# Slot parameters normalised in the embedding, expert row scales in two rounds, attention's masks and first loads behind the gathers, the recurrence output's loads inside the recurrence

## What is computed

```python
h = base_weight[ids]; h = where(id is tuned, train_weight[row], h)          # embedding
h = h + attention(layernorm(h))          # 12 heads of 16, column 0 masked for all rows but 0
h = h + switch_ffn(layernorm(h))
# test-time-training layer, 12 heads of 64, chunks of 16 tokens:
for each of the 32 chunks:               # W, b are the state of each head
    grad = ln_l2_bwd(k @ W + b, v - k);  W -= (last_eta * k).T @ grad;  b -= ...
    out = q + layernorm(q @ W - (eta * tril(q k.T)) @ grad + b - (eta * tril) @ grad)
h = h + (layernorm(out) * gelu(x @ wg)) @ wo
# soft mixture of 32 experts with 32 slots each:
xn   = l2norm(layernorm(h));  phin = scale * phi / max(norm of phi over its 192 rows, 1e-12)
d_w  = softmax(xn @ phin over slots);  c_w = softmax(xn @ phin over all 1024)
h = h + c_w @ experts(d_w.T @ xn)
```

## Time and profile before

| | us |
|---|---|
| median of 3 runs | 1601.47 |
| lowest, highest | 1600.15, 1617.8 |
| the profiled execution, device time | 1609.5 |
| its span in the trace | 1607.7 |

### The profile page before, as it was taken

How to read it: one execution, slowest core, us unless ns; L and a number is a source line. 1 busy time by engine, 2 the same in 40 slices (tenths; PEclk the granted TensorE clock), 3 DMA queues, 4 the chain that set the end, 5 groups by cost and what they waited for, 6 DMA issues and landing times. The chain is left out here.

```text
span 1607.7 us, 28934 instructions
## 1 busy us (share of the span) xinstructions
PE 1337.4 (83%) x10025; PEld 930.0 (58%) x10025; DVE 904.1 (56%) x2168; ACT 758.6 (47%) x1536; POOL 359.1 (22%) x378
## 2 busy tenths in 40 slices
PE   0939999699489993989999948989758887898979
PEld 0503333346257772677777736767654433798879
DVE  4448885412577771777686849787845766000001
ACT  0406556221234441788797925767632332333333
POOL 7230000000167773344343420000001223000000
PEclk9959999659789997899999979999966999899989
DMA  2351120000313334333333343212023000399941
GB/s 54 94 92 51 54 57 21 23 1 0 89 42 119 119 119 124 91 106 103 111 98 109 100 105 85 57 48 55 1 67 81 0 1 0 94 261 244 262 111 39
DMA packets 113496, 132.12 MB, mean 82 GB/s; under 512 B 27871, under 2 KB 99278, under 8 KB 113272
## 3 DMA queue, kind: packets, MB, share of 16 engines
...
...
## 5 line engine op out<-in xcount | busy, mean ns | idle before, releaser
L561 DVE TENSOR_REDUCE mx<-bank 128x1 f32<-128x512 f32 x192 | 119.6, 681 | 35.1 <-PE bank L483 34.8
L621 ACT ACTIVATE PT<-bank 128x1024 f32<-128x1024 f32 x96 | 94.3, 1022 | 85.6 <-PE bank L499 84.9
L2181 POOL TENSOR_TENSOR m_cw<-m_E,m_f 128x1024 f32<-128x1024 f32 x16 | 45.1, 2817 | 381.9 <-DVE m_f L2126 381.9
L2266 DVE TENSOR_TENSOR x_eo<-bank,b 128x192 f32<-128x192 f32 x32 | 11.4, 357 | 173.1 <-PE bank L2243 173.1
L2232 PE MATMUL bank<-slT,w 96*128 x768 | 97.6, 287 | 13.3 <-DMA b<-in_m_b 9.3
L1552 POOL TENSOR_SCALAR r_grD<-gr 32x192 f32<-32x192 f32 x128 | 68.5, 535 | 173.1 <-DVE gr L1455 152.1
L1334 PE MATMUL bank<-r_grD,ek 128*128 128x256 f32 x384 | 105.2, 412 | 0.0
L2232 PEld LDWEIGHTS bank<-slT,w 96*128 96x128 f32 x768 | 93.8, 201 | 17.8 <-issue 17.8
L2254 ACT ACTIVATE x_g<-bank,w 128x128 f32<-128x128 f32 x192 | 53.0, 375 | 105.5 <-PE bank L2232 105.5
L483 PE MATMUL bank<-K,Q 97*128 97x512 bf16 x192 | 70.0, 418 | 28.2 <-POOL K L636 24.9
L1334 PEld LDWEIGHTS bank<-r_grD,ek 128*128 128x128 f32 x384 | 70.9, 198 | 13.7 <-issue 0.7
...
## 6 DMA issues: line engine op xcount, KB each, us to landing
...
```

What stands on the lines that cost most here:

```text
L561: v.tensor_reduce(mx[u % 2][:, j // 4, j % 4:j % 4 + 1], slot(f"A{u}.{j}"), AX.X, ALU.max).then_inc(*dve.did(f"max{u}.{j}"))
L621: a.activation(PT[kt % 2][:, 2 * hp:2 * hp + 2, :], STB[s % 2][:, :, :], ACT.Exp, scale=DH ** -0.5)\
```

## The change

**Embedding.** Two loads of `m_phi` and one of `m_scale` are issued behind the weights, and the normalisation of `phi` is done here with the same operations as before in dispatch (ACT squares and root, 16 matmuls, 8 spreading matmuls, four DVE products); the result is stored to a new DRAM tensor `phin_d`. DVE's part stands between `tuned` and `layer_norm(0)`. ACT takes one square root ahead, so that the table is loaded early. The first `train(0)` comes before `base(2)`. Behind its last gather POOL writes attention's mask rows. SP issues the 36 loads of attention's units 0 to 2 behind the stores of sequence 1 and ahead of those of sequences 2 and 3, and no longer waits at the end for the stores of the sequences to land (attention waits for them where it loads).

**Preparation and recurrence.** `W0`, `B0`, `g2` come as three whole loads in the preparation, and DVE centres them at its end. In the recurrence POOL fills two key tiles first instead of zeroing all four; PE and ACT start each half by itself. SP's loop is written out; the loads of steps past the end are gone but for one. SP loads there what the output needs: mask tables ahead of the steps, parameters behind step 0, three tiles behind steps 26 to 28, biases behind steps 27 to 30. DVE zeroes the output's tiles and builds its masks before the first step (before, POOL zeroed them, at the output's start).

**Dispatch.** SP loads `phin_d` instead of `m_phi`. Statistics and row scales are computed for sequence 0 alone and then for the other three; `units(1)` and `units(2)` move into the loop, to tiles 1 and 5.

The heart of the diff:

```diff
@@ embed, SP
+                for k in range(KC):
+                    sp.dma_start(phi[:, k, :], ins["m_phi"][k * DC:(k + 1) * DC, :]).then_inc(phi_in, 16)
+                sp.dma_start(scale[:, :], ins["m_scale"]...).then_inc(phi_in, 16)
...
+                for k in range(KC):
+                    sp.wait_ge(normed, k + 1)
+                    sp.dma_start(M["phin_d"][k * DC:(k + 1) * DC, :], phi[:, k, :]).then_inc(phi_out, 16)
                 for b in SB:
+                    if b == 2:
+                        sp.wait_ge(stored[0], 16 * 2 * QUADS)
+                        for u in C:
+                            attention_rows(sp, M, u)
...
-                for r in range(2):
-                    sp.wait_ge(stored[r], 16 * 2 * QUADS * B // 2)
+                sp.wait_ge(phi_out, 32)
@@ embed, DVE, behind tuned
+                v.wait_ge(rooted, 1)
+                v.tensor_scalar(size[:, :], size[:, :], FLOOR, None, ALU.max).then_inc(united, 1)
...
+                v.wait_ge(spread, 1)
+                for k in range(KC):
+                    for hf in range(2):
+                        cols = slice(hf * SL // 2, (hf + 1) * SL // 2)
+                        last = v.tensor_tensor(phi[:, k, cols], phi[:, k, cols], QK[hf][0:DC, :], ALU.mult)
+                    last.then_inc(normed, 1)
@@ embed, POOL
                 base(0)
                 base(1)
+                train(0)
                 base(2)
-                train(0)
@@ attention, PE
-                t_.wait_ge(masks, QUADS)
@@ ttt_recur, SP
-                with sp.Fori(0, STEPS // SPT) as sc:
+                for s in range(STEPS):
...
+                    if s + RING <= STEPS:
                         sp.wait_ge(*dve.at(f"gx1.{j}", sc))
                         targets(r, nx)
...
+                    if s + RING < STEPS:
                         sp.wait_ge(*pe.at(f"upd1.{j}", sc))
                         keys(r, nx)
...
+                    if s in (26, 27, 28):
+                        t = s - 26
...
+                            sp.dma_start(O["Wd"][t][rr, :, rr], M["W_d"][t, rr, :, 0, :]).then_inc(O["tiles_in"][t], 16)
+                            sp.dma_start(O["Gs"][t][:, hh, :], M["g_d"][0, hh, t * P:(t + 1) * P, :]).then_inc(O["tiles_in"][t], 16)
+                    if s in (27, 28, 29, 30):
+                        t = s - 27
...
+                                sp.dma_start(O["b6"][r0:r0 + HP, t, :, hh * E1:(hh + 1) * E1],
@@ ttt_recur, PE
-                t_.wait_ge(primed_k, 3)
-                t_.wait_ge(primed_w, 2)
-                before(0, 0).then_inc(first_z, 1)
+                t_.wait_ge(primed_k, 1)
+                t_.wait_ge(primed_w, 1)
+                before(0, 0).then_inc(first_z, 1)
@@ moe_dispatch, DVE
+                sizes(0, slice(0, TB))
                 units(0)
...
-                units(2)
+                sizes(1, slice(TB, TILES))
                 for i in I:
+                    if i == 1:
+                        units(1)
+                    if i == TB + 1:
+                        units(2)
```

445 lines of the change are left out of this document (228 added, 217 removed).

## The result

The changed kernel takes 1553.86 us (median of four runs, 1551.44 to 1560.38). The kernel before took 1606.73 us beside it (four runs, 1600.15 to 1617.8). The ratio is 0.9688, with a 95% interval of 0.9613 to 0.9764. The medians differ by 52.9 us. The two profiled executions took 1609.5 and 1560.38 us and differ by 49.1 us, where the prediction had 62.2.

A forecast was written before the change was run, and what follows sets the result against it. Five idle gaps of 5 to 25 us at block starts, adding in full, were taken as removable: 16.9 + 14.0 + 4.9 + 13.0 + 13.4 = 62.2 us. On the median 1601.47 that gave 1540 us, range 1532 to 1555.

The forecast's parts named there:

- The embedding's gain of 16.9: Embedding to attention's first matmul: sequences 5.5 us earlier, SP decides the end, first matmul at 87.3 instead of 104.2.
- the cost of 0 for the recurrence's steps: Recurrence loop: steps stay at 8.10 us, SP's added loads land in time; bound 1 us at each of five steps.
- Masks beside work: Embedding: POOL's mask memsets follow its last gather at about 52, done by 69, beside other work.
- 1.6 us a stretch: Embedding: memsets would stretch scalings of sequences 2 and 3 by 1.6 us each, sum unchanged since SP decides.
- Preparation, 0: Preparation's end: three DMAs and some 3.5 us of DVE work hidden under SP's last stores; 3.5 without that cover.
- Recurrence's start, 14.0: Recurrence block's start: tables land at 628, first variance at 631.1 instead of 645.60; gain 14.0, bounds 10 and 17.5.
- the bound of 10: Recurrence's start: lower bound of the gain, if tables come 4 us later behind 1.2 MB of state loads.
- Recurrence's end and output's start, 4.9 + 13.0: Recurrence ends at 934.3 instead of 939.24; output's first square comes 10.3 us into its block instead of 23.3.
- The upper bound, a higher granted clock: Output's start: gain up to 15, since after a short idle time PE's clock may still be at the higher level.
- Dispatch's start, 13.4: First logits 14.4 us sooner, less 1.0 for units(1); gain 10.6 if units(2) is not absorbed.
- the likeliest case: Whole kernel: the forecast itself, 1534 to 1546 us, chance 0.54.
- one start stays: Rival, chance 0.13: another wait replaces a removed one, likely at recurrence or output; price 10 to 13 us, 1552.

The follow-up runs named there:

- first pair: The first profiled executions of the kernel before and the changed kernel, no further edit: 1609.5 and 1560.38 us.
- before: The kernel without the change: median 1606.73 us beside the changed kernel.
- after: The kernel with the change described above and no further edit: median 1553.86 us, ratio 0.9688 against the kernel before.
- group 1: Runs on one chip: both kernels once more, masks moved back behind attention's block, and no normalisation of phi; the kernel before took 1614.58 us in one run.
- group 3: Runs on one chip: changed kernel once more (1566.09 us), padding in embedding gaps, row tables first, and all four edits together.
- groups 2, 4 and 5: Runs sharing a chip within each group: 2 gathers, masks, loads, padding; 4 added gathers, repeats, three mends; 5 three mends with padding, and the kernel before (1595.84 us).
- again_after: Changed kernel once more, no edit, second profile: 1563.52 us, ratio 0.9746 against the kernel before.
- masks_late: Changed kernel with the mask memsets back at the start of attention's block, PE waiting for them: 1586.52 us, ratio 0.9877.
- half_gathers: Changed kernel without the last eight of 32 gathers (tuned rows of sequences 2 and 3): 1550.15 us in one run.
- after_fourth: Changed kernel once more, no edit, beside the added-gathers run: 1548.83 us, ratio 0.97 against the kernel before.
- second pair: Two later profiles of the same two kernels, on two different chips; attention starts at 104.14 and 88.91 us, the difference sums to 49.6 us.
- gathers_attn: Changed kernel with 192 more gathers on POOL during attention, into a tile nobody reads: 1664.92 us, ratio 1.0443.
- idx_first: Changed kernel with the output's four mask-table loads ahead of targets and keys in the recurrence's block: 1556.74 us, ratio 0.9736.
- no_phi: Changed kernel without the normalisation of phi, so dispatch gets it unscaled: 1548.69 us, ratio 0.9638.
- pad32: Changed kernel with 32 unused one-column matmuls in the embedding, where PE waits for phi's squares: 1553.7 us, ratio 0.9788.
- pad_gaps: Changed kernel with two lots of 16 unused one-column, 16-row matmuls in gaps of the embedding: 1569.22 us, ratio 0.9787.
- best: Changed kernel with four edits: masks paced by sequence 3's scaling, attention loads split, padding in embedding gaps, mask tables first: 1561.2 us, ratio 0.9708.
- lean_pad: Changed kernel with masks paced, loads split, tables first, plus 32 unused matmuls at the end of the preparation: 1531.77 us, ratio 0.9606.
- loads_split: Changed kernel with attention's 36 loads split, 12 ahead of sequence 1's stores and 24 ahead of sequence 2's: 1548.03 us, ratio 0.9722.
- best_lean: Changed kernel with masks paced by sequence 3's scaling, loads split, tables first, no padding: 1535.94 us, ratio 0.9646.

## Why the prediction was right or wrong

**What failed, in short.** The gaps and their releasers were read rightly, and four of the five starts came as forecast or within 3 us. Two steps failed. The embedding's gain of 16.9, by which all sequences follow 5.5 us earlier in a chain, was absent in the first pair, where TensorE and ACT issue late by 15.6 us; why they do is open. And the cost of 0 for the recurrence's steps was 4.1 to 10.7 us. The gain of 10.7 us in the experts' stage, which no step had, covers part of this.

**What bounds the kernel.** Right: five gaps at block starts, in a row, each with its releaser. All five could be closed or shortened. What was wrong is that the work between them keeps its length.

**Embedding, 16.9 forecast: nearly right without the slow issue, absent in the first pair.** Without the slow issue it is 15.2 (104.14 to 88.91), with first matmul at 88.91 against the forecast's 87.3. SP decides, as the step said: loads to 79.17 (forecast 78.4), stores to 87.8 (86.7); the last 1.1 us are the meeting of the engines at the block's border, for which the step had 0.6. The last `phi` product ends at 28.25 (forecast 27.5). With the slow issue in both kernels the gain is 8.6 (112.89 to 104.25); with it in after alone it is nothing. The step that failed in the first pair is the sentence that the other sequences "follow in a chain" 5.5 us earlier: from about 31 us to 53, TensorE and ACT issue ever more slowly in the profile of after and in two of the five groups, and the first store comes at 60.04, not 48.19. There was no row for it, as the profile of before is of an execution without it. Between the two profiles of after, 11.9 us are there at the first store, 15.1 at the end of sequence 1's stores (76.9 against 61.8), and 15.6 at the first matmul (104.56 against 88.91).

What causes it stays open. In all four profiles of group 1, both of after and before among them, it is there, and so in group 3; it is in none of groups 2, 4 and 5, group 4 having run on the chip of group 3. Neither `phi`'s normalisation nor the masks bring it about, and before has it without either. It starts while the gathers are issued and ends at 52.8 to 56.1 us, about when the last has landed (53.1 to 53.4 by POOL's wait); more TensorE instructions in that stretch make it longer (26.55 us of ACT idle in the padded kernel). The two runs meant to vary the gathers fell into groups without it. The timed medians of after by group, 1563.5 and 1566.1 with it, 1548.8 without, fit its price, and so do those of before (1606.2 and 1603.7 with it, 1593.9 to 1595.1 without it, for a price of 8.7). The first pair doesn't fit in as well: before has 1606.7 with a profile that is free of it, and after 1553.9 with one that has it. The groups differ in their chips, too. So the medians suggest that it isn't an effect of profiling, but do not show it.

**Masks beside work.** The prediction placed them there at no cost. Without the slow issue it was right: they meet the scaling of sequence 3, hidden behind SP. With it they meet that of sequence 2, 6.58 us instead of 1.25, and 7.31 in again_after. That costs the stage 1.3 us by masks_late, so it is a small part of what the embedding lost; where POOL comes to the masks sooner, as in half_gathers, attention starts 4.4 us later than in the kernels beside it. The prediction's sentence from the Trainium skill (SBUF — State Buffer, practical consequences) expected 1.6 us a stretch, sized by one slow row of the dispatch loop. By the Trainium skill's rule itself, that the later engine waits for the whole instruction, four scalings can each wait for a memset of 1.80 us, 7.2 in all. The trace agrees with this reading of it: the four operations of after_fourth take 1.39, 1.94, 1.97 and 1.94 us. The 1.25 of masks_late agrees too; it was my sizing that was wrong.

**Preparation, 0.** Right in mechanism: DVE's last operation ends 14.3 us ahead of the recurrence's block in before and 10.6 in after, while POOL's ends 12.0 ahead in both. From attention's first matmul to the block it is 515.1 before and 514.3 after (515.0 and 516.0 in the second pair). This stretch of stages takes 508.9 to 516.9 us over 19 profiles, gathers_attn left aside, so a cost of a few us could not have been seen in its length.

**Recurrence's start, 14.0: 11.9.** Right in mechanism: DVE waits for SP's tables, the case that the bound of 10 was made of. The term mis-sized is the landing of the fourth table. Forecast at 628, it let DVE go on at 630.67: issued at 623.26, it let DVE go on 7.4 us later, behind the four loads of targets and keys. The forecast had taken "the 5.65 us of the earlier trace rows or somewhat less", and no row stood behind the "somewhat less": with 5.65 in full, from the start of the issue, its own sum gives about 630. idx_first took this wait away and gained 4.4 more.

**The steps, 0: -4.1 to -10.7.** This is the step of the prediction that failed whatever the chip. It put the term at 0 because it asked only whether SP's added loads come in time; they do, and steps of 8.1 us between the turnovers stay 8.1. It did not ask what a changed number of TensorE instructions ahead of the loop does to the loop. The steps of after's placement cost 2 to 12 us more than before's, nearly all of it behind the turnovers, and 0.5 to 1.4 us at half-step 7 in eleven of the twelve profiles. Five profiles with a shifted placement (no_phi, pad32, pad_gaps, best, lean_pad) took 286.0 to 289.2 us, twelve with after's placement 289.6 to 300.1 (the lowest is half_gathers, the next 291.9), and three of before 287.4 to 288.0. That the placement decides is shown by the padding, three times at different places with the same end, and by the torn matmuls, there in all twelve and in none of the other eight. By the estimate in group 3 most of the loss is then paid at the lower granted clock, which lasts longer behind the turnovers. That the tearing comes about through the packets of instructions, which meet the snapshot's stores, is how I read the DMA view; no run varied the stores. And no run changes the clock without the placement, so what keeps it low is not shown. Against this loss stands a gain of about 0.4 us at each of four half-steps (4.43 before, 4.08 after), not forecast either.

**Recurrence's end and output's start, 4.9 + 13.0: 17.6.** Right; the two can't be told apart after, since the block's border has no row of its own. The upper bound, a higher granted clock, brought nothing that can be told from it: the clock fell to 0.50 here too, from 928.5 to 935.3. The output's stage itself became 1.2 us longer (232.3 against 231.1, in twelve of the 17 profiles of changed kernels), which was not forecast. The granted clock goes with it. In before it stays at 1.00 for the stage's first 196 us; in after it is at 0.50 for 6.8 us, from 1106.0 to 1112.8, and a tile there takes 17.7 us instead of 15.8. In the three profiles of changed kernels without such a fall (loads_split, idx_first, best_lean) the stage takes 229.0 to 229.1. What brings the fall about is open.

**Dispatch's start, 13.4: 13.8, and 11.5 in the second pair.** The first logits come 14.5 us sooner after the block's start (forecast 14.4). From there to the first `m_cw` it is 15.1 us in after and 14.1 in before, at a granted clock of 0.73 and 0.74, so `units(1)` and the other statistics cost the 1.0 that was counted. From the second `m_cw` on each tile but the last takes 9.4 us in both, that of `units(2)` too. The 2.8 us that the prediction put against this part, if `units(2)` is not absorbed, were not lost in the first pair. In the second pair the sum is 11.5 although the first logits come 15.2 sooner: the rest of the stage took 147.6 us in that profile of before, where the clock was already at 1.00 from the first logits to the first `m_cw`, which took 11.3 us; it took 150.5 in the first, and 151.2 in after_fourth.

**Experts: not in the forecast.** Their code is the same, and they took 161.3 us in the profile of before and 150.5 in that of after. Over 19 of the 20 profiles, that of best left aside, this stage takes from 143.8 to 165.9 us, in both kernels: 161.3, 165.9 and 151.3 in before alone. The costliest groups of the two pages and of after_fourth, first before:

```profile
L2232 PE MATMUL bank<-slT,w 96*128 x768 | 97.6, 287 | 13.3 <-DMA b<-in_m_b 9.3
```

```profile
L2265 PE MATMUL bank<-slT,w 96*128 x768 | 93.7, 280 | 8.5 <-DMA b<-in_m_b 3.3
```

```profile
L2265 PE MATMUL bank<-slT,w 96*128 x768 | 92.4, 279 | 3.3 <-ACTq L45 2.0
```

After the second | stand PE's idle time and what of it ended with a weight's bias load: 9.3, 3.3 and, in the third, so little that it isn't named. The stage moves 38.9 MB in each, at 241 GB/s in the first and 258 in the second, and the DMA engines are busy for 0.96 and 0.97 of it. But the loads aren't all of it. Here is the stage of before and then of after, columns as above:

```profile
1391.89:1553.24 161.35, 150.02 (x1091) 145.35 (x1090) 11.08 (x31) 58.63 (x187) 0.00 (x0) 0.97 0.96 241
```

```profile
1353.35:1503.83 150.48, 144.02 (x1091) 140.38 (x1090) 11.09 (x31) 58.64 (x187) 0.00 (x0) 1.00 0.97 258
```

Of the 10.9 us between them 6.0 are busy time of PE and 4.8 its idle time, and the granted clock is 0.97 in one and 1.00 in the other. What part each has is not shown. So the 10.7 of the first pair's 49.1 us are not shown to be any work of the change: stages with the same code differ by as much between two profiles of one kernel. Without this entry it had brought 38.4 there, and 43.2 in the second pair.

**The number.** The range of 1532 to 1555 holds the measured 1553.86, by 1.1 us; the likeliest case, 1534 to 1546, doesn't, and the first pair has 38.4 of the forecast's 62.2 without the 10.7 of the experts' stage. So that it lies inside is luck. The rival "one start stays" (1552) gave the right time, and in the profile of after one start did stay, but at the embedding and by neither of the waits that it named; that is luck too. Both signs by which the prediction wanted to be called wrong came about: the steps changed their length by more than 2 us, and at the recurrence's start DVE has a new idle time that ends with a DMA (6.28 us, `o_idx`). The sign was never in doubt: of the four comparisons of after with before, the ratio nearest to 1 was 0.9754.
